# Gated attention: the block maxima move ahead of the projections, and the attention values go last in each unit

## The reference

```
ss = sigmoid(x @ Ws); sd = sigmoid(x @ Wd)           # (b, t, H=8, E=5)
ms, md = top-3 masks of ss and sd over the 5 experts
q5 = x @ Wq ; k5, v5 = x @ Wkv                       # (b, t, H, E, 64)
q = sum_e q5 * sd * md ; k = sum_e k5 * ss * ms ; v = sum_e v5 * ss * ms
attn = softmax(q k^T / 8) ; out = attn v             # per head, 1024 x 1024
y = sum_e ((out @ Wo)_e * md_e) ; x = layernorm(x + y)
```

## Time and profile before

| what | value |
|---|---|
| three runs | 4691.93, 4693.07, 4693.48 us; median 4693.07 |
| the profiled execution | 4695.17 us; its span, first to last instruction, 4693.4 us |
| PE, PEld busy over the span | 88%, 46% |
| DVE, ACT, POOL busy | 74%, 42%, 59% |
| mean granted PE clock over the span | 0.943 |

### The profile page before, as it was taken

One profiled execution on the slowest core, in us unless ns is written; L12 is line 12 of the kernel. 1 busy time (PEld: TensorE's weight loads), 2 busy tenths in 40 slices (PEclk: granted clock), 3 DMA queues, 4 the chain that ended last, 5 costly groups with the idle time before them and its releaser, 6 DMA issues. The chain is left out here.

```text
span 4693.4 us, 63371 instructions
## 1 busy us (share of the span) xinstructions
PE 4113.2 (88%) x22554; PEld 2146.0 (46%) x22554; DVE 3458.5 (74%) x5816; ACT 1969.6 (42%) x3446; POOL 2788.1 (59%) x2036
## 2 busy tenths in 40 slices
PE   5999999999868999989999848999999999999964
PEld 3554454544445555555555424444444444444423
DVE  3877887878667777777877637887888788878836
ACT  2443443434445445445454313444344344434422
POOL 0655655556625677776786915665666566656640
PEclk6999999999978999999999958999999999999987
DMA  2000000000020000000000021211112111112111
GB/s 51 13 14 13 23 13 22 14 9 5 1 71 18 26 26 26 27 26 26 31 26 9 5 58 24 39 30 28 36 28 41 28 37 28 31 25 45 18 46 36
DMA packets 98041, 125.90 MB, mean 27 GB/s; under 512 B 28896, under 2 KB 76448, under 8 KB 97728
## 3 DMA queue, kind: packets, MB, share of 16 engines
q1 hardware_dynamic: 97728, 121.86, 11.8%
HBM read 103.69 MB, written 18.12 MB: 26 GB/s over the span
## 5 line engine op out<-in xcount | busy, mean ns | idle before, releaser
L729 POOL TENSOR_TENSOR s_psum_p<-s_psum_p,s_prob 128x1024 f32<-128x1024 f32 (+3 forms) x640 | 1350.2, 2110 | 415.5 <-ACT s_prob L476 376.7
L476 ACT ACTIVATE s_prob<-s_sT 128x1024 f32<-128x1024 f32 (+2 forms) x896 | 835.9, 933 | 970.4 <-DVE s_sT L610 479.8
L384 PE MATMUL s_pv<-s_prob,s_vp 128*64 128x512 f32 (+3 forms) x3584 | 889.0, 575 | 3.9 <-POOL s_prob L714 3.0
L729 POOL TENSOR_TENSOR s_psum_p<-s_prob 128x1024 f32<-128x1024 f32 (+1 forms) x128 | 286.9, 2241 | 573.5 <-ACT s_prob L476 570.8
L615 DVE RECIPROCAL s_recip<-s_recip 128x128 f32<-128x128 f32 x512 | 480.8, 941 | 99.3 <-ACT s_recip L426 99.3
L340 PE MATMUL s_mx<-s_bh,s_ah 64*128 64x512 f32 (+3 forms) x1792 | 390.7, 431 | 183.0 <-DVE s_bm L551 84.6
L1613 POOL TENSOR_TENSOR s_psum_p<-s_psum_p,s_prob 128x1024 f32<-128x1024 f32 x192 | 464.3, 2418 | 111.4 <-ACT s_prob L1340 109.5
L561 DVE CUSTOM_DVE_ANT_0 s_mx<-s_mx,s_strip 128x512 f32<-128x512 f32 x640 | 429.1, 711 | 111.9 <-PE s_mx L340 110.9
L1340 ACT ACTIVATE s_prob<-s_sT 128x1024 f32<-128x1024 f32 x256 | 262.6, 1026 | 478.0 <-PE s_sT L1200 474.1
L1455 DVE SCALAR_TENSOR_TENSOR s_part<-s_sT,s_gate,s_part 128x128 f32<-128x128 f32 x945 | 287.4, 322 | 213.1 <-ACT s_part L1332 180.6
L359 PE MATMUL s_sT<-s_ah,s_bh 64*128 64x512 f32 (+3 forms) x1792 | 414.4, 459 | 19.1 <-ACT s_prob L476 18.8
(11 more groups left out here) (251 smaller groups left out, 7560.4 us busy)
## 6 DMA issues: line engine op xcount, KB each, us to landing
s_strip<-bias_rows SPq DMA_DIRECT2D x256, 144.0 KB, 5.7
s_wr<-gated_weights SPq DMA_DIRECT2D x32, 960.0 KB, 4.8
s_near<-bias_rows SPq DMA_DIRECT2D x256, 48.0 KB, 2.0
x<-s_x SPq DMA_DIRECT2D x12, 512.0 KB, 3.2
s_x<-x SPq DMA_DIRECT2D x8, 512.0 KB, 4.7
gated_weights<-s_side_hi SPq DMA_DIRECT2D x8, 480.0 KB, 2.5
gated_weights<-s_side_lo SPq DMA_DIRECT2D x8, 480.0 KB, 2.9
s_x<-in_L_attn_x_dram SPq DMA_DIRECT2D x4, 512.0 KB, 4.3
```

Of the source, the lines that this page charges most:

```text
L384: last = mm(pv[heads(hd), lo:CH], vp[:, g % 2, j, heads(hd)], prob[:, k % PR, hd, lo:CH], start=j == 0, stop=end)
L476: nc.scalar.activation(prob[:, k % PR, :, lo:CH], sT[:, k % 2, :, lo:CH], ACT.Exp, scale=st.scale).then_inc(exp_done, 1)
L729: nc.gpsimd.tensor_tensor(out[:, :, lo:CH], src, p[:, :, lo:CH], ALU.add)\
```

## The change

In every unit of the gated stage:

- PE before: scores, first projection step, chunk (two where the unit has no step), values of unit k - 2, second step, first odd job, other chunks, other odd jobs. PE after: scores, chunk (or two), all steps, all odd jobs, values of unit k - 2, other chunks.
- DVE before: late jobs, steps, chunks. DVE after: late jobs, the chunk (or two) that PE does first, steps, other chunks.
- ACT: the copy of `pv` comes one unit later (unit 2 in place of 1, unit 10 in place of 9), and ahead of the steps of its unit.

```diff
@@ tail_pass
-            if u == 1 and k > 1:
+            if u == 2 and k > 2:
                 return 2 * (k // U) - 1
-            return 2 * (k // U) if u == st.at1 + 1 else None
+            return 2 * (k // U) if u == st.at1 + 2 else None
@@ tensor
                 chunks = [t for t in todo if t[0] == "mx"]
-                for t in steps[:1]:
-                    project(t[1], t[2], k)
                 early = 1 if steps else 2
                 for t in chunks[:early]:
                     maxima(t[1], t[2], second(todo, t, k))
+                for n, t in enumerate(steps):
+                    project(t[1], t[2], k if n == 0 else None)
+                for t in todo:
+                    if t[0] in GMISC:
+                        misc_job(t)
                 if k >= 2:
                     values(k - 2)
-                for t in steps[1:]:
-                    project(t[1], t[2])
-                odd_jobs = [t for t in todo if t[0] in GMISC]
-                for t in odd_jobs[:1]:
-                    misc_job(t)
                 for t in chunks[early:]:
                     maxima(t[1], t[2])
-                for t in odd_jobs[1:]:
-                    misc_job(t)
@@ scalar
                 exponentials(k)
-                steps = [t for t in todo if t[0] == "pj"]
-                for t in steps[:1]:
-                    project(t[1], t[2], k)
                 if tail_pass(k) is not None:
                     copy_values(tail_pass(k))
-                for t in steps[1:]:
-                    project(t[1], t[2])
+                steps = [t for t in todo if t[0] == "pj"]
+                for n, t in enumerate(steps):
+                    project(t[1], t[2], k if n == 0 else None)
@@ vector
+                steps = [t for t in todo if t[0] == "pj"]
+                chunks = [t for t in todo if t[0] == "mx"]
+                early = chunks[:1] if steps else chunks[:2]
+                for t in early:
+                    maxima(t[1], t[2], second(todo, t, k))
+                for n, t in enumerate(steps):
+                    project(t[1], t[2], k if n == 0 else None)
                 for t in todo:
-                    if t[0] == "pj":
-                        project(t[1], t[2], k if t is todo[0] else None)
-                    elif t[0] == "mx":
-                        maxima(t[1], t[2], second(todo, t, k))
+                    if t[0] == "mx":
+                        if t not in early:
+                            maxima(t[1], t[2])
```

## The result

The change makes the kernel faster: 4660.0 us, median of four runs (4659.5 to 4662.7), where before takes 4693.3 (4691.9 to 4695.7). The ratio is 0.993, 95% interval 0.9913 to 0.9947, so 33 us less; the forecast was 4668, in a range from 4654 to 4695. The profiled execution takes 4659.7, its span 4658.0 where before had 4693.4: 35.4 less. From the first scores of the stage to its last the difference is 39.6 (1418.1 to 2692.0 before, 1423.5 to 2657.8 after). The other 4 us lie in stages whose code is the same, and I put them down to the variation from one run to the next.

A forecast was written before the change was run, and what follows sets the result against it. PE was taken to bound the stage (busy 1168 of 1271 us), with idle time and a fallen clock besides. Terms -4 + 8 - 9 - 6 - 19 = -30, clock +4, gave -26: 4667 from 4693, stated as 4668, range 4654 to 4695.

The forecast's parts named there:

- (a): Units 0 to 3: new order of PE's groups takes 0.09 us less a unit, 46 times: -4 us.
- (b): Units 4 and 6 to 9: chunk ahead delays the step, so the loop goes from 4.53 to 4.76 us: +8 us.
- (c): Units that PE fills (unit 5, some unit 10, some with gates, y, t): 31 units by 0.3: -9 us.
- (d): Units 9 to 11, where PE waits for DVE: earlier chunks give -6 us in eight pairs, -19 in six others.
- (e): ACT's copy of `pv`, units 2 and 10: delays DVE's step by some 0.4 us, covered by spare time: nothing.
- The clock: Units 10 and 11: some three clock falls without PE's wait behind rs remain, at about 1.3 us each: +4 us.
- The wait that I blamed: Units 10 and 11: PE's wait of 0.5 to 1.2 us behind rs, present at six of eight falls, goes.
- The clock falls oftener: Rival, chance 0.13: PE's larger gaps in units 4 and 6 to 9 lose the clock; slower, +14 us, 4707.
- The gain of units 9 to 11 isn't kept: Rival, 0.19 (not kept or halved): six pairs' work waits elsewhere as DVE is the bound; sum -7 us, 4686.
- The loop is dearer: Rival, inside the 0.68 for faster: step 0.43 late in units 4, 6 to 9, +17 to +20; sum -15, 4678.

The follow-up runs named there:

- e3: Changed kernel, but in units 0 to 9 the first step stands ahead of the first chunk again on PE and DVE: 4666.6 us, ratio 0.9938.
- e5: Changed kernel, but first step ahead of first chunk in units 4 and 6 to 9, save those with job y or t: 4655.1 us, ratio 0.9908.
- e4: Kernel before, with only DVE's order changed: it reduces the chunk before its step, PE still makes the step first: 4795.4 us, ratio 1.0213.
- e7: Changed kernel, but ACT copies the values ahead of the exponential in units 2 and 10: 4652.9 us, ratio 0.9909.
- the second profile: Profile of the changed kernel run once more, unaltered, beside the other experiments: 4668.2 us, ratio 0.9935.
- e9: Changed kernel, but the row sums (rs) issued behind the values, not ahead, in units 5 and 10: 4683.4 us, ratio 0.9969.
- e6: Kernel before, but in units 10 and later PE and DVE take the first chunk ahead of the step: 4683.4 us, ratio 0.9969.
- e1: Changed kernel, but in every unit the first step stands ahead of the first chunk again on PE and DVE; values stay last: 4709.4 us, ratio 1.0031.
- e8: Kernel before, but PE issues the row sums (rs) ahead of the values in units 5 and 10: 4706.5 us, ratio 1.0013.
- e10: Changed kernel with both the edits of e5 and e7: 4653.9 us, ratio 0.9905.
- e11: Changed kernel, but the row sums (rs) issued between chunk and step in units 5 and 10: 4697.5 us, ratio 1.0005.
- e2: Changed kernel, but values right behind the first step and ACT's copy where it was before; chunk still first: 4689.6 us, ratio 0.9986.

## Why the prediction was right, point by point

**(a) Units 0 to 3.** Predicted 0.09 less a unit, measured 0.18. Each spacing that I gave is there: step to step 0.23, item to values 0.53, values to scores 1.01. The missed 0.1 is inside the second step: from its start to the item it takes 1.40 behind values, but 1.30 behind the first step, and its first matmul 0.47 and 0.36. The end of unit 3 of pair 9:

```profile
2185.54 0.39 PE L1135 MATMUL s_sT<-s_wr,s_xh 128*128 128x512 f32 x1
2185.77 0.36 PE L1133 MATMUL s_mx<-s_wr,s_xh 128*128 128x448 f32 x1
...
2187.07 0.60 PE L1068 MATMUL s_misc<-constants,s_qkv 128*128 128x128 f32 x4
2187.60 1.08 PE L1212 MATMUL s_pv<-s_prob,s_qkv 128*64 128x512 f32 x4
2188.61 0.50 PE L1195 MATMUL s_sT<-s_ah,s_bh 64*128 64x512 f32 x2
```

**(b) The loop.** 4.76 as predicted, in all of units 6 to 9 without another load, with DVE's chunk ahead of its step and PE's gap at 0.82 (0.78 was said). e3 and e5 take it away again, e4 shows what sets it. The price of +8 holds: the units 4 and 6 to 9 in which the clock is full in both kernels add up to +9, those with y and t included.

**(c) Units that PE fills.** Unit 5 gave 0.41 and unit 10 0.40, for 0.3 predicted; as in (a), the rest is inside the groups that now stand behind their like, the chunk behind the scores and rs behind the step (1.84 us for 1.95). But the units with y gave nothing: unit 7 of pairs 5, 9 and 13 takes 6.64 for 6.0, and the next 4.76 for 5.5. Together about -9, as said.

**(d) Units 9 to 11.** In the regular pairs with full clock (5, 9, 13) 0.77 over units 11 and 12, for 0.74 in unit 11. Pairs 0, 3 and 7: 3.6, 3.8 and 2.7 for 3.0, 3.9 and 3.0; pair 1: 2.7 for 3.2. Pairs 4 and 8 are the miss: 1.0 for 2.9. I took it that the step is ready for DVE ahead of the next unit; but behind the ranking DVE now does chunk and step in unit 9, and PE stalls before the scores of unit 10 (units 9 and 10 of pair 8):

```profile
2132.22 0.98 DVE L1472 TENSOR_TENSOR s_keep<-s_keep,s_beats 128x256 f32<-128x256 f32 x1
...
2133.12 1.21 DVE L1493 TENSOR_REDUCE s_bm<-s_mx 128x2 f32<-128x1024 f32 x1
2134.25 1.62 DVE L1449 SCALAR_TENSOR_TENSOR s_part<-s_sT,s_gate,s_part 128x128 f32<-128x128 f32 x5
...
2135.97 0.50 PE L1195 MATMUL s_sT<-s_ah,s_bh 64*128 64x512 f32 x2 [1.90 <-issue]
2137.01 0.69 PE L1200 MATMUL s_sT<-s_mr,s_rowsel 64*128 64x512 f32 x2
```

Unit 9 is 0.4 longer, and the clock falls after the stall, so that unit 10 lasts 7.4, where it had 7.3.

**(e) The copy of `pv`.** Nothing in pairs 1 to 13, which e7 confirms. For pairs 14 and 15 "nothing" was wrong: their units 1 and 2 got some 5 us longer together, a part of it a fallen clock. PE waits for the item behind DVE's layer norm, and for the copy that now comes a unit later. The item starts at +3.4 in unit 1 of pair 14 in both kernels; before, the values filled 1.1 us of that wait, and now they stand behind it:

```profile
2562.14 0.66 PE L1068 MATMUL s_misc<-constants,s_qkv 128*128 128x128 f32 x4 [2.19 <-DVE s_al L1393]
...
2568.00 1.08 PE L1212 MATMUL s_pv<-s_prob,s_qkv 128*64 128x512 f32 x4 [0.96 <-ACT s_z L1257]
```

In these short units the cover of 2 us, which I had read from the full ones, isn't there.

**The clock.** This is the term that failed, in its sign. I gave +4, by falls counted behind rs with and without a wait; the time at the low level went down by 47 us, by 37 in the second profile. What that is worth I can only bound. A fall of 3.4 us in unit 6, which PE nearly fills, costs 1.5 (0.45 for each us); in units 11 and 12 it mostly costs 0.5 to 0.9 (0.15 to 0.25), since DVE holds them up anyway, though pair 11 of e9 pays 2.5 for 6.8 us there (0.37). So 47 us are some 7 to 21 of the 39.6. From the other side: the measured lengths put (a) at -8, (b) at +9, (c) at -9 and (d) at -21, together -29 for the forecast -30, and pairs 14 and 15 are 1.5 shorter. That leaves about 9 of the 39.6, an estimate of what the clock gave back.

The wait that I blamed, 0.5 to 1.2 us behind rs, is not the cause. In e6 these waits before the second chunk of unit 10 are gone, only waits of 0.35 to 0.49 are left around the start of unit 11, and the clock falls at nine rs of unit 10, not at eight. In e1 it falls at 12 of 13 rs of unit 5, and PE waits for nothing there. e9 and the changed kernel have the same waits in unit 11 and differ by 51 us at the low level. The longer wait of the earlier trace rows is another matter: PE waits 1.74 to 1.88 us in unit 11 eight times (before, e1 and e8), and seven times the clock falls 1.5 to 2.1 us behind its end, in the kernel before in unit 12 of pairs 2, 11 and 12. The change takes that wait away, and these falls with it.

Why the neighbours of rs matter isn't shown, nor whether it is the chunk or something that goes with it. One such thing is how often the form of the matmuls changes in the unit (see the last section): three times in unit 5 of the changed kernel, of e5, e7 and e10, four or five times in the other orders. Only e11 speaks against it, which has three changes there and falls all the same.

**The rivals.** *The clock falls oftener*: not by the loop. PE idles 0.82 of 4.76 in units 6 to 9, and no unit there had a clock under 1.00, save unit 9 of pairs 1 and 14, of which pair 1 has a stall of 3.8. The rule of the Trainium skill, page "TensorE: Matmul & The Clock Gate", section "A second HAM failure mode: psum-queue depth-cycling", by which frequent small pauses make the clock go up and down, did not come true for these pauses. As a mechanism the rival did exist, in the row sums: e1 and e8 are slower than before by it. *The gain of units 9 to 11 isn't kept*: wrong, units 10 to 12 keep it. Only pairs 4 and 8 bear it out, and the start of pair 4: its units 0 and 1 are 1.5 us longer than before, behind a stall of 4.59 us for 3.83, and so take back a part of what pair 3 gained. *The loop is dearer*: no, 4.76.

The total was right within 8 us partly by luck, then: the pairs 4, 8, 14 and 15 cost some 9 us that I did not have, and the packing and the clock gave more than that.

## What to carry to other kernels

Put a borrowed buffer's step first where the next unit waits for that buffer, and the other engine's small work first where TensorE is full or the other engine is late; one order for all units loses in one of the two (e10 is 14 us faster than the changed kernel beside it, and e5's stage 10 us shorter). Move the orders of both engines together: moving VectorE's alone cost 100 us. Keep groups of like matmuls side by side, for each change of form cost 0.2 us here, and look at what stands next to a group with nearly no columns.

## What the runs showed of the hardware

Each change of form between neighbouring groups of matmuls cost about 0.2 us. The rows give the form: scores and chunk are 64*128, step, rs and the other jobs 128*128, values 128*64. Unit 5 has the same instructions in every order and, in these kernels, no wait of PE between its scores and the next. With three changes up to the next scores (chunk, step, rs, values: the changed kernel) it takes 5.54; with four (chunk, step, values, rs: e2 and e9) 5.75; with five (step, chunk, rs, values: e1, e3 and e8; step, chunk, values, rs: before) 5.94. Unit 10 goes the same way, 5.89, 6.08 and 6.28. In e5 and e10 unit 5 takes 5.67 with three changes: DVE reads the chunk of unit 4 until +0.9 there, and the step starts at +1.48 where the changed kernel has +1.36. Units 0 to 3 went from four to three, and from 5.58 to 5.40. A part of it shows in single rows: the first matmul of a step takes 0.36 behind a step and 0.47 behind scores, chunk or values.

The granted clock depended on the order of instructions around sixteen one-column matmuls (1.84 to 1.95 us): 0 to 3 us at the low level in units 5 and 6 in five profiles of one order, 10 to 41 in the nine profiles of the others, while repeated gaps of 0.82 in 4.76 us left it at its full level.
